# A decoder layer on one core: the order of four matmul items in the hand-written schedule of a step

## The reference

```python
x = layernorm(x + attn(x))                  # self attention, ALiBi bias, no mask
x = layernorm(x + xattn(ctx, ctx, x, mask)) # cross attention to ctx, 16 x 120 x 256
x = layernorm(x + ffn(x))                   # 8 experts of 1024, top 2 of a softmax gate
# attn:  q, k, v = x @ W.T + b; softmax(q k / 4 + bias) v; @ Wo.T + bo
# xattn: the same with W not transposed, keys masked by mask * -1e9
```

## Time and profile before

| what | value |
|---|---|
| time of three runs, us | median 1414.84 (1407.99 to 1415.6) |
| the profiled execution, us | 1412.27 |
| its span, us | 1410.2 |
| PE, DVE, ACT, POOL busy, share of the span | 77%, 72%, 40%, 34% |
| a step of the first kind (203.0 to 246.4), us | 43.40 |
| a step of the second kind (519.85 to 565.08), us | 45.23 |

### The profile page before, as it was taken

The page is one execution under the profiler, slowest core; times in us unless marked ns, Lnnn a source line. Parts: engine busy times, 40 slices in busy tenths (PEclk is TensorE's granted clock), DMA queues, the critical chain, the costliest instruction groups (busy, mean ns, idle before and its releaser), DMA issues. The chain is left out here.

```text
span 1410.2 us, 32514 instructions
## 1 busy us (share of the span) xinstructions
PE 1091.7 (77%) x9874; PEld 772.1 (55%) x9875; DVE 1022.0 (72%) x2410; ACT 567.4 (40%) x1022; POOL 483.5 (34%) x597
## 2 busy tenths in 40 slices
PE   3778899889888888888885600088999999999980
PEld 2445666666655655565553400066777777777750
DVE  2579999999888989999985340066777777777764
ACT  1344555555545656665563200022323323332324
POOL 1233433433344343534322037612223223223324
PEclk7799999999999999999997555599999999999995
DMA  8489886678756887788754152275222222222227
GB/s 207 108 225 226 230 200 142 157 180 227 174 108 163 235 237 154 207 232 221 202 168 137 68 194 106 100 267 159 42 43 43 41 45 41 41 45 41 43 30 245
DMA packets 160383, 202.20 MB, mean 143 GB/s; under 512 B 30444, under 2 KB 141692, under 8 KB 157067
## 3 DMA queue, kind: packets, MB, share of 16 engines
q1 hardware_dynamic: 145864, 182.92, 48.7%
q0 software_dynamic: 13296, 17.83, 7.5%
q10 hardware_dynamic: 1152, 0.53, 0.2%
HBM read 122.63 MB, written 74.41 MB: 140 GB/s over the span
## 5 line engine op out<-in xcount | busy, mean ns | idle before, releaser
L1177 PE MATMUL HB<-xhi,W 128*128 128x128 f16 x2272 | 292.1, 221 | 21.7 <-issue 16.1
L1177 PEld LDWEIGHTS HB<-xhi,W 128*128 x2272 | 202.2, 98 | 65.8 <-issue 48.2
L1177 PE MATMUL HB<-xlo,W 128*128 128x128 f16 x1136 | 225.0, 220 | 0.0
L1460 POOL DMA_INDIRECT d_sums<-ysc,tok x71 | 111.0, 1563 | 327.3 <-DMA XB<-d_rows 171.7
L892 ACT ACTIVATE PT<-SB 128x1024 f32<-128x1024 f32 x128 | 131.1, 1024 | 138.3 <-PE SB L563 136.3
L659 DVE TENSOR_REDUCE mneg<-SA 128x4 f32<-128x1024 f32 x128 | 156.5, 1223 | 41.6 <-PE SA L515 39.5
L1177 PEld LDWEIGHTS HB<-xlo,W 128*128 x1136 | 111.9, 99 | 50.2 <-issue 0.7
L1370 DVE SCALAR_TENSOR_TENSOR hlo<-HB,hhi 128x512 f16<-128x512 f32 x142 | 98.2, 691 | 55.1 <-ACT hhi L1238 51.1
L1238 ACT ACTIVATE hhi<-HB 128x512 f16<-128x512 f32 x142 | 84.2, 593 | 121.3 <-DVE HB L1362 121.2
L1362 DVE SCALAR_TENSOR_TENSOR HB<-HB,SC,b1c 128x512 f32<-128x512 f32 x142 | 107.1, 754 | 16.7 <-PE HB L1177 11.9
L1246 ACT ACTIVATE ysc<-yb,wv 128x256 f32<-128x256 f32 x71 | 36.1, 508 | 191.8 <-DVE yb L1394 181.6
(11 more groups left out here) (195 smaller groups left out, 2500.4 us busy)
## 6 DMA issues: line engine op xcount, KB each, us to landing
wst<-in_w SPq DMA_DIRECT2D x32, 1024.0 KB, 10.0
d_w<-w SPq DMA_DIRECT2D x16, 1024.0 KB, 6.7
W<-d_w SPq DMA_DIRECT2D x8, 2048.0 KB, 8.7
k_stack<-d_k SPq DMA_DIRECT2D x96, 128.0 KB, 7.2
XB<-d_rows SPq DMA_DIRECT2D x71, 130.0 KB
d_rows<-fill SPq DMA_DIRECT2D x4, 1950.0 KB, 15.6
d_q<-q_part SPq DMA_DIRECT2D x16, 384.0 KB, 5.8
d_k<-k_part SPq DMA_DIRECT2D x16, 384.0 KB, 2.7
```

What stands on the lines that cost most here:

```text
L1177: mm = pe.matmul(out, w.rearrange("p e n -> p (e n)"), x[n % 2][:, k, :], start=(k == 0 and half == 0 and x is xhi), stop=(k == KT - 1 and ...
L1460: pool.indirect_dma_start(YS, bass.IndirectOffsetOnAxis(ap=tok[n % 6][:, 0:1], axis=0), ysc[n % 2][:, :], None, compute_op=ALU.add).then_i ...
```

## The change

AOTc moves from (2,1) to (2,0) and Oc from (3,1) to (3,0); Vc moves from (2,0) to (2,1) and K from (3,0) to (3,1). `ITEMS`, the order in the second bank, has Oc ahead of K accordingly. No item is added or dropped, and no other code changes: all engines read their places from these two tables.

```diff
-             [("Qc", -1), ("Vc", -1), ("K", 1), ("Oc", -2), ("V", 1), ("O", 0), ("R", -2)]]
+             [("Qc", -1), ("Vc", -1), ("Oc", -2), ("K", 1), ("V", 1), ("O", 0), ("R", -2)]]
...
-    GAPS = {(0, 0): ("Q", 1), (0, 1): ("T1", -1), (1, 0): ("Qc", -1), (2, 0): ("Vc", -1),
-            (2, 1): ("AOTc", -2), (3, 0): ("K", 1), (3, 1): ("Oc", -2), (4, 1): ("Kc", 0),
+    GAPS = {(0, 0): ("Q", 1), (0, 1): ("T1", -1), (1, 0): ("Qc", -1), (2, 1): ("Vc", -1),
+            (2, 0): ("AOTc", -2), (3, 1): ("K", 1), (3, 0): ("Oc", -2), (4, 1): ("Kc", 0),
             (5, 1): ("V", 1), (6, 0): ("T2", -2), (6, 1): ("AOT", 0), (7, 0): ("O", 0), (7, 1): ("R", -2)}
```

## The result

| kernel | median us (lowest to highest, runs) | ratio to before, 95% interval |
|---|---|---|
| before | 1414.57 (1407.99 to 1415.6, 4) | |
| after | 1492.1 (1488.96 to 1495.18, 4) | 1.0553 [1.0519, 1.0587] |

The change makes the kernel slower by 5.5%, 77.5 us. The forecast was 1451 us, in a range of 1425 to 1468: the sign is right, the size is wrong by 41 us, and the time lies outside the range.

What follows compares the result with a forecast made beforehand. VectorE's chain sets a step, TensorE close behind. Steps 2 to 7 add 18.2 us, 8 to 14 16.3, step 15 0.8, step 0 3.2, step 1 0.3: 38.8 on 1412.27 gives 1451 us, range 1425 to 1468.

Steps and rivals of the forecast that it cites:

- Part 1: Unit 2: AOTc ahead of scores (2,1) waits for its norm, making maximum (3,0) 1.73 us late, bounds 1.3 to 2.1.
- the five terms behind the wait: TensorE from 216.77: AOTc and keyed 0.93, scores and keyed 0.97, weigh 1.00, Vc 0.97, scores to maximum 0.64; 4.51 us.
- Part 2: Unit 3: Oc takes K's place ahead of scores (3,1), K goes behind; saves 0.90 us a step, at least 0.66.
- The hole ahead of r: VectorE's idle 0.66 us before the residual sum at 225.71, said to go when Oc moves up.
- Part 3: K's later chain: POOL's split of K starts 6.0 us later in a step; costs 3.2 us once, in step 0.
- the circle: Loop from k_stack's landing through scores, maxima and d_k to the next scores: 44.6 us, against a step of 43.4.
- rival 2: k_stack's landing sets the step, every POOL delay entering that loop: 1468 us, chance 0.13.
- nothing on it in steps 1 to 14: The k_stack loop was charged no time in these steps, being shorter than the step the other terms make.
- Part 4: VectorE's casts and copies in units 4 to 6 stand under POOL's block: +2.2 us a max step, +1.5 a halve step.
- Rival 1: Only the stall counts, POOL's collisions being traded one for one: 15 us more, 1427 us, chance 0.17.
- rival 3: AOTc finds its norm ready and Oc's better place remains: 19 us faster, 1393 us, chance 0.05.
- rival 4: Nothing to measure: slack between engines takes up the 0.83 us a step and K's chain lies hidden; chance 0.05.

Runs made afterwards that it cites:

- the first experiment: Kernel before with only AOTc moved to (2,0) and Vc to (2,1), K and Oc left in place: 1460.35 us, ratio 1.0316.
- the filled wait: Changed kernel with eight extra unread matmuls, half of an earlier try's sixteen, ahead of AOTc in its wait: 1466.23 us, ratio 1.0377 to before.

## Why the prediction was right in its sign and wrong in its size

**Part 1 failed, at "From 216.77 on the path is TensorE's".** The wait was right: 2.14 us at the named place, with maximum (2,1) behind an idle VectorE, and 1.67 us a step where the clock held (1.73 forecast). But the five terms behind the wait were taken from rows of the kernel before, in which TensorE had not just stood still. In the trace after, from AOTc's start to Vc's are 3.92 us (235.97 to 239.89) where the full clock takes 2.44 (183.48 to 185.92 in the first experiment). The lacking term is 1.8 to 2.1 us a step, 26 us in all, shown by the filled wait. The stated bounds of 1.3 and 2.1 held only the full clock.

**Part 2 failed at most of its size.** The hole ahead of r went as said. That the step gains 0.90 left out that K writes the bank that VectorE reads Oc from, directly behind it: 0.89 us of wait on TensorE, and the turning of maxima queued behind K, 0.68 idle on VectorE. The gain is 0.12 instead of 0.90. K in the other bank gives 0.9 as forecast. The prediction named what is queued behind AOTc, but did not ask the same of K. This is worth 8 to 10 us.

**Part 3 was right for the middle, too small at the start.** K's split came 7.3 us behind maximum (3,1) (6.3 forecast). In steps 1 to 9 the scores (0,0) of the changed kernel start 0.05 to 0.63 us behind k_stack's landing, the circle at its limit. In steps 3 to 8 VectorE is busy until its maximum (0,0) all the same, so there rival 2 did not decide. Ahead of this maximum in steps 1, 2 and 9 it stands idle for 4.64, 0.75 and 1.95 us (before 0, 0 and 0.12), so that "nothing on it in steps 1 to 14" was wrong for these three. The last of them, for the scores that k_stack released:

```profile
470.03 1.23 DVE L659 TENSOR_REDUCE mneg<-SA 128x4 f32<-128x1024 f32 x1 [1.95 <-PE SA L515]
```

Step 0 cost 4.4 us (3.2 forecast) and step 1 3.0 (0.3 forecast), the wait at the start of step 1 being

```profile
76.95 1.01 PE L515 MATMUL SA<-k_stack,q_stack 99*128 99x256 bf16 x4 [6.03 <-DMA k_stack<-d_k]
```

where 1.61 us was the earlier trace rows. The scores behind it take 1.01 us instead of 0.60; here too the clock is down (0.50 from 77 to 80 us). That it makes up the rest of step 1 is argued from this row and not tried alone.

**Part 4, the term said to decide, was right in max steps; in halve steps its number came right and its reason did not.** D grew by 1.92 / 1.32 us where +2.2 / +1.5 was forecast. In a max step the small instructions stand 2.1 us longer than before, and the order of POOL moves them. The subtraction that meets x1bo takes 1.27 us for 0.17, so the trace agrees again with the rule of the Trainium skill that the prediction cites. In a halve step the small instructions stand only 0.1 us longer (4.4 before, 4.5 after), and the weight instruction L771 takes 0.4 more in D; VectorE's waits in D grew by 0.7, from 0.56 ahead of a copy mts to 1.26 ahead of V's addition. This addition in step 12 after:

```profile
663.76 0.69 DVE L723 TENSOR_TENSOR V<-BK,rows_b 128x512 f32<-128x512 f32 x1 [1.31 <-PE BK L433]
```

and in step 11 before, with no wait:

```profile
554.89 0.68 DVE L723 TENSOR_TENSOR V<-BK,rows_b 128x512 f32<-128x512 f32 x1
```

With the half filled wait, D of a halve step is 22.27, only 0.66 more than before: about half of the 1.32 goes with the clock. That 1.32 is near 1.5 is therefore luck.

**The rivals.** Rival 1 (no net lock) is excluded by the stretched instructions of the max steps, rival 2 by the middle steps, rival 3 by the wait, rival 4 by all. The fallen clock was in none of them, so that the 0.90 for slower was good and the range was not.

The account, for the profiled executions (1412.27 and 1489.04, +76.8): the sum of the prediction 38.8; the clock 6 x 1.79 + 7 x 2.11 = 25.5; K's bank 13 x 0.78 = 10.1; steps 0 and 1 more, 3.9; stretch A 6 x 0.19 = 1.1; D less than forecast, 6 x 0.28 + 7 x 0.18 = 2.9 off; together 76.5, taking step 8 as one of the halve steps. Step 8 added only 3.4 where these added 5.0, what lies behind step 14 added 2.6 where 0.8 was said, and step 0 starts 0.7 later; these three are not explained, and their sum is small. Most of the 1.1 of stretch A is step 2, where k_stack landed late and A grew by 0.9.

## What to carry to other kernels

A wait on TensorE costs up to about its length (1.18 us for 1.09, 1.67 for 2.15) and then, if the granted clock falls behind it, the longer time of the matmuls that the next engine is waiting for (scores 1.06 us for 0.60): price the instructions behind a new wait at both clock levels, and try the same order with a shorter wait or with work put into it. When items that share a bank change places, ask for each one who reads the bank ahead of it at that moment and what is queued behind it, as for every other wait. And measuring the change with the lacking terms taken away tells more about a forecast than the total does, if it is compared stretch by stretch: here 40.8 us for 38.8 hides a halve step that is short by 0.6 and a step 1 that is over by 4.3.

## What the hardware showed that was not expected

The same wait of 2.15 us, in the same kernel (the first experiment), brought the clock to 0.50 in steps 4 and 6 and left it at 1.00 in steps 3 and 5. With AOTc behind Vc, the waits of 1.09 us left it at 1.00 in all steps 2 to 7, and those of about 1.6 us in steps 9 to 14 left it there in B; elsewhere in these steps it was at 0.50 for 2.8 us a step (1.7 before). What decides between the two is not shown by these runs. Stretch B in steps 2 to 7 of the first experiment takes 7.0, 8.6 or, at 0.50 for twice as long, 9.9 us and nothing between, and a mean over many steps is needed to price such a place. And work whose result nobody reads, put into the wait, made the kernel faster by 26 us.
